# The last experts' rows transposed by DMA from SyncE instead of by TensorE and VectorE

## The reference

```python
x = x + _L0_xattn_ref(_layernorm(x), ctx_1024, ...)
x = x + _L0_ffn_ref(_layernorm(x), ...)
x = x + _L1_xattn_ref(_layernorm(x), ctx_1024, ...)
x = x + _L1_ffn_ref(_layernorm(x), ...)

def _L1_ffn_ref(x, router_w, router_b, w1, b1, w2, b2):
    x_flat = x.reshape(-1, Dx)
    probs = jax.nn.softmax(x_flat @ router_w.T + router_b, axis=-1)
    topk_prob, topk_idx = jax.lax.top_k(probs, K)          # K = 2
    y = jnp.zeros_like(x_flat)
    for e in range(E):                                      # E = 8
        gate = jnp.sum(jnp.where(topk_idx == e, topk_prob, 0.0), axis=-1)
        h = jax.nn.gelu(x_flat @ w1[e].T + b1[e])
        out = h @ w2[e].T + b2[e]
        y = y + gate[:, None] * out
```

## Time and profile before

| | |
|---|---|
| median of 3 runs | 703.61 us (700.66 to 711.06) |
| the profiled execution | 701.29 us, of which the span is 699.6 us |
| busy in the span | PE 550.0 us (79%), DVE 540.8 (77%), POOL 378.3 (54%), ACT 375.6 (54%) |
| the last mixture's slots | first turn at 462.5 us, last scatter issued at 688.7 us |

### The profile page before, as it was taken

How to read it: one execution, slowest core, us unless ns; L and a number is a source line. 1 busy time by engine, 2 the same in 40 slices (tenths; PEclk the granted TensorE clock), 3 DMA queues, 4 the chain that set the end, 5 groups by cost and what they waited for, 6 DMA issues and landing times.

```text
span 699.6 us, 17811 instructions
## 1 busy us (share of the span) xinstructions
PE 550.0 (79%) x6572; PEld 499.8 (71%) x6572; DVE 540.8 (77%) x1063; ACT 375.6 (54%) x556; POOL 378.3 (54%) x324
## 2 busy tenths in 40 slices
PE   6799999999997614897770655159999999999990
PEld 5798989898995503776550444159999999999990
DVE  3678999999997773887655898768888888888860
ACT  1665577777765513997642677305444444444440
POOL 8057698889887306654307883043444554444331
PEclk9899999999998955999995799559999999999996
DMA  8300111212121235897745342421333233333221
GB/s 295 123 2 23 40 56 60 63 54 75 40 77 51 76 122 158 254 315 232 200 145 176 106 111 71 137 61 22 54 51 48 47 48 53 55 48 49 32 27 21
DMA packets 38756, 64.35 MB, mean 92 GB/s; under 512 B 7665, under 2 KB 28786, under 8 KB 38418
## 3 DMA queue, kind: packets, MB, share of 16 engines
q1 hardware_dynamic: 27442, 42.71, 19.2%
q0 software_dynamic: 11232, 20.50, 15.4%
HBM read 45.74 MB, written 17.45 MB: 90 GB/s over the span
## 4 chain that ended last, share of the span: by engine, by line
PE 49%; DVE 22%; issue 7%; DMA 7%; ACT 7%; POOL 5%; DVEq 1%; SPq 0%; ACTq 0%; POOLq 0%
PE banks L1334 46%; DMA sorted_y<-slot_region 3%; POOL rv L526 2%; PE banks L1543 2%; DVE w_region L972 1%; DVE heads L964 1%; DVE slot_region L1212 1%; DMA staging<-w_t 1%; ACT w_region L639 1%; DVE heads L947 1%; DVE w_region L954 1%; DVE w_region L977 1%; DVE w_region L926 1%; POOL wb_region L601 1%; DVE x_res L1279 1%
## 5 line engine op out<-in xcount | busy, mean ns | idle before, releaser
L1334 PE MATMUL banks<-w_region 128*128 128x128 f16 (+6 forms) x1964 | 163.9, 242 | 21.2 <-DVE w_region L1142 9.1
L1334 PEld LDWEIGHTS banks<-w_region 128*128 128x128 f16 (+3 forms) x1964 | 150.0, 118 | 30.4 <-issue 10.2
L614 POOL DMA_INDIRECT out<-slot_region,lg x39 | 65.0, 1667 | 114.4 <-ACT slot_region L823 111.4
L1334 PE MATMUL banks<-w_region,wb_region 128*128 (+1 forms) x1000 | 119.8, 277 | 6.8 <-DMA wb_region<-wk 6.7
L1334 PEld LDWEIGHTS banks<-w_region,wb_region 128*128 128x128 f16 (+1 forms) x1000 | 100.7, 107 | 17.4 <-issue 7.5
L1334 PE MATMUL banks<-slot_region,staging 128*128 128x128 f16 x1872 | 113.1, 221 | 0.1
L785 ACT ACTIVATE wb_region<-wb_region 128x1024 f32<-128x1024 f32 x39 | 41.3, 1058 | 133.0 <-DVE wb_region L1194 133.0
L1334 PEld LDWEIGHTS banks<-slot_region,staging 128*128 128x128 f16 x1872 | 108.5, 99 | 0.2 <-issue 0.2
L1185 DVE COPY staging<-w_region 128x2048 f16 x78 | 60.1, 773 | 35.8 <-PE banks L1334 34.3
L570 POOL DMA_INDIRECT slot_region<-normed_rows,index x46 | 48.1, 1045 | 48.9 <-DVE index L1157 20.5
L1334 PE MATMUL banks<-wb_region,w_region 128*128 (+1 forms) x344 | 50.4, 296 | 13.6 <-DVE slot_region L1212 13.4
(11 more groups left out here) (244 smaller groups left out, 1052.8 us busy)
## 6 DMA issues: line engine op xcount, KB each, us to landing
staging<-w_t SPq DMA_DIRECT2D x24, 512.0 KB, 4.7
sorted_y<-slot_region SPq DMA_DIRECT2D x23, 256.0 KB, 5.6
w_region<-w_t SPq DMA_DIRECT2D x8, 512.0 KB, 5.5
x_res<-x SPq DMA_DIRECT2D x4, 512.0 KB, 9.9
staging<-w_in SPq DMA_DIRECT2D x4, 512.0 KB, 3.7
normed_rows<-w_region SPq DMA_DIRECT2D x16, 128.0 KB, 1.7
staging<-w_out SPq DMA_DIRECT2D x4, 512.0 KB, 3.7
gated_rows<-wb_region SPq DMA_DIRECT2D x16, 128.0 KB, 2.3
```

The source lines that it names most:

```text
L614: g.indirect_dma_start(out=out, out_offset=bass.IndirectOffsetOnAxis(ap=back[:, j:j + 1], axis=0), in_=m.y[:, j % m.YB, 0, :], in_offset=N ...
L1334: return t.matmul(o, a, b, start=start, stop=stop)
```

## The change

The transpose of step 2 is taken from TensorE and VectorE. SyncE issues four DMA transposes for each slot instead, each of one 128 x 128 piece of f16 (32 KB), from the gathered home straight into `m.xT`, which now has three homes (`XB`) in place of two; the gathered rows have seven homes in place of eight and lie behind `m.xT` in the region. SyncE waits for the slot's gather, and from slot 3 on for the end of up of three slots before, whose home it writes. TensorE's up waits for a new semaphore per home (`slot_turned`), VectorE computes the gates as soon as the gather has landed (`slot_gate`), and POOL reuses a home of gathered rows when its gates are computed and its transposes have landed. The first mixture keeps its transposes on TensorE.

```diff
-            m.RING, m.AHEAD, m.YB = ((3, 2, 3), (8, 4, 4))[layer]
-            m.rows, at = carve(SLR, 0, [m.RING, m.A, (2 * D, ROW1)[layer]], F16)
-            m.xT, at = carve(SLR, at, [2, 2 * DC, m.SW], F16)
+            m.RING, m.AHEAD, m.YB = ((3, 2, 3), (7, 4, 4))[layer]
+            m.XB = (2, 3)[layer]
+            m.xT, at = carve(SLR, 0, [m.XB, 2 * DC, m.SW], F16)
+            m.rows, at = carve(SLR, at, [m.RING, m.A, (2 * D, ROW1)[layer]], F16)
...
+        def turned(j):
+
+            n = moes[1].XB
+            return sem(f"slot_turned{j % n}"), 16 * 2 * DC * (j // n + 1)
...
             sp.dma_start(rows_v[1][:, :, D:D + 2].bitcast(F32).rearrange("t p k -> p t k"), token_gates).then_inc(sem("gates_kept"), 16)
+            sp.wait_ge(sem("gates_kept"), 16)
+            m = moes[1]
+            for j in range(m.NSLOT):
+                sp.wait_ge(*gathered(1, j))
+                if j >= m.XB:
+                    sp.wait_ge(*up_done(1, j - m.XB + 1))
+                for c in range(2 * DC):
+                    sp.dma_start(m.xT[:, j % m.XB, c, :], m.rows[:, j % m.RING, 0, c * P:(c + 1) * P],
+                                 transpose=True).then_inc(turned(j)[0], 16)
+            sp.wait_ge(sem("y_scattered"), 16 * NSLOTS[1])
...
-                        pool.wait_ge(sem("slot_cols" if layer else "slot_tr"), made(layer, j - m.RING + 1))
+                    if j >= m.RING and layer == 0:
+                        pool.wait_ge(sem("slot_tr"), j - m.RING + 1)
+                    elif j >= m.RING:
+                        pool.wait_ge(sem("slot_gated"), j - m.RING + 1)
+                        pool.wait_ge(*turned(j - m.RING))
...
-            def slot_cols(j):
+            def slot_gate(j):
                 m = moes[1]
-                dve.wait_ge(sem("slot_tr"), made(1, j + 1))
-                if j >= 2:
-                    dve.wait_ge(*up_done(1, j - 1))
+                dve.wait_ge(*gathered(1, j))
...
-                       in1=pair[:, 0:1], op0=ALU.mult, op1=ALU.add)
-                v.tensor_copy(m.xT[:, j % 2], slot_columns(m, j)).then_inc(sem("slot_cols"), 1)
+                       in1=pair[:, 0:1], op0=ALU.mult, op1=ALU.add).then_inc(sem("slot_gated"), 1)
...
-                pe.wait_ge(sem("slot_cols"), made(1, j + 1))
+                pe.wait_ge(*turned(j))
...
-                xT, ps = m.xT[:, j % 2], hidden(m, j)
+                xT, ps = m.xT[:, j % m.XB], hidden(m, j)
...
-                        slot_tr(layer, s)
+                        if layer == 0:
+                            slot_tr(layer, s)
```

More of the change, by code:

```diff
@@ L566, in gather_rows @@
                 for a in range(m.A):
-                    if j >= m.RING:
-                        pool.wait_ge(sem("slot_cols" if layer else "slot_tr"), made(layer, j - m.RING + 1))
+                    if j >= m.RING and layer == 0:
[3 more added lines that the diff above has]
+                        pool.wait_ge(*turned(j - m.RING))
                     q = m.A * j + a
@@ L1245, in slots_of_last @@
                             slot_weights(0, a)
-                        slot_cols(0)
+                        slot_gate(0)
                     elif s + 1 < n:
-                        slot_cols(s + 1)
+                        slot_gate(s + 1)
                         expert_at(s + 1)
```

## The result

The changed kernel takes **714.7 us** (median of 4 runs, 713.84 to 718.91) against 704.08 of the kernel before in the same comparison: a ratio of 1.0137, 95% interval 1.0093 to 1.0180. It was forecast at 695 and is slower. The profiled execution has a span of 713.2 us, 13.6 more than before.

A forecast was written before the change was run, and what follows sets the result against it. TensorE was taken to be full and to bound the last mixture's slots. The sum was 701.29 - 8.1 (transposes off TensorE) + 1.5 (start) = 694.7 us, predicted as 695, with a range of 692 to 712.

The forecast's parts named there:

- the price of a transpose: SyncE in the last mixture's slots: about 0.45 us per DMA transpose, so a slot's four occupy 1.8 of 5.30 us.
- t: Time of one DMA transpose on SyncE, taken as about 0.45 us; four must fit in 5.30 us, 1.33 each.
- the transposes set the pace: Rival: over 1.33 us per transpose, slots go at SyncE's pace; beyond 1.34 slower than before; 788 us at 1.9. Chance 0.17.
- The 696.5: Estimated total in place of 694.7 if a DMA transpose takes the skill's 1309 ns, four taking 5.24 us.
- Transposes off TensorE: Last mixture's slots: 0.22 us of turns leaves the path 37 times, 8.1 us gained, a slot taking 5.30 for 5.52.
- nothing is gained: Rival: the 0.22 us return as a wait between down and up, leaving only the start's loss, 703 us. Chance 0.05.
- The copy off VectorE: 39 copies of 0.41 us leave VectorE, which has slack in each slot: worth nothing on the path.
- The start: First up of the last mixture waits for four transposes: 1.5 us later, bounds 0.8 to 5.5.
- Latency covered by three homes: Transposes have 13.2 us between issue and use, transfers land after 1.9 to 5.0: covered after the first slots.
- The scatters as a rival: Transposes on the shared DMA engines delay POOL's chained scatters, which then set the slots' pace: 709 or 731 us. Chance 0.12.
- x: Time the transposes add to each scatter's landing; slots then go at 4.5 + x, over 5.52 us beyond x = 1.0.

The follow-up runs named there:

- e1: Changed kernel with a slot's four transposes issued as one instruction of 128 x 512: 696.28 us, ratio 0.9915 to the kernel before.
- e2: Changed kernel with six homes for turned rows in place of three, and eight for gathered rows: 716.34 us, ratio 1.016 to the kernel before.
- e4: Kernel before, with its TensorE turns kept, plus the 156 DMA transposes into homes that no engine reads: 707.02 us, ratio 1.0057 to the kernel before.

## Why the prediction was wrong

**The step that failed** is the price of a transpose. The prediction took "about 0.45 us, the row of the same size on the same queue", for t. Measured is 1.24 us at the median and 1.42 from one to the next. The row it was taken from the earlier trace rows shows plain copies, and a transpose on the same queue holds SyncE almost three times as long. The bounds held it (0.32 to 1.9), and so did the rival *the transposes set the pace*, which put the turning point at t = 1.34 and had a chance of 0.17. By its formula the last slot is turned at 462.5 + 156 x 1.42 = 684.0, and the last up did begin at 685.26. That the two lie so close is in part chance, since the last four ups wait for no transpose.

The margin was thin, and by this working two parts of t were needed to cross it. At 1.234 + 0.04 us, four transposes are 5.10 us, still under 5.30. The 25 longer ones add 21.4 / 39 = 0.55 us to a slot, which makes 5.65 (measured 5.67). That TensorE waits before 17 ups only fits this; no run has four transposes per slot without any fetch. The prediction did not have the program's fetches at all.

The Trainium skill, VectorE: DVE Perf Modes, section "The three transpose paths", has 1309 ns for a 128 x 128 transpose of bf16 by DMA. The trace agrees in size: 1234 ns of issue at the median, for f16. By that figure alone, as an estimate, four take 5.24 us, under the 5.30 of the matmuls, and the kernel would have gained; the longer transposes, of which the section says nothing, turned that. The 696.5 that the prediction gives for this figure does not follow its own terms: with 462.5 + 3 x 1.309 + 2.3 = 468.7 the start is 4.1 us later, and the sum 697.3. And it is no price by area, since 128 x 512 took 1190 ns.

*Transposes off TensorE: 8.1 us.* Right. In e1 up of slot 3 begins at 480.25 and up of slot 38 at 665.75, 5.30 us a slot; in the kernel before it was 5.52. The step of 5.31 us in the earlier trace rows was the right one to read, and the rival that nothing is gained falls with e1.

*The copy off VectorE: nothing.* Not tested by itself. In e1 the chain in the steady slots does not touch VectorE.

*The start: 1.5 us.* Too small, for the same reason. The first four transposes go out from 462.31 to 466.07, 1.25 us apart instead of 0.44, and up begins 2.98 us after the last, at 469.05, **4.4 us** later than the 464.64 of the earlier trace rows. The landing was also longer than the 2.3 us taken. In e1, with one instruction, the first up begins at 465.20, 0.6 us later. The rows of the changed kernel and of e1:

```profile
469.05 4.20 PE L1350 MATMUL banks<-slot_region,staging 128*128 128x128 f16 x48 [11.08 <-DMA slot_region<-slot_region]
```

```profile
465.20 4.36 PE L1349 MATMUL banks<-slot_region,staging 128*128 128x128 f16 x48 [7.51 <-DMA slot_region<-slot_region]
```

*Latency covered by three homes.* Right, by e1: with three homes no up but the first waits for a transpose, and it is SyncE that waits, up to 4.9 us. In e2 SyncE had no wait for a home, so six homes could not show it.

*The scatters as a rival.* They do not set the pace. By the rule of the Trainium skill, DMA: Bandwidth & Descriptors, section "Issuing engines are not separate DMA queues", x should be above zero. In e4 the median landing rises from 3.9 to 4.0 us and the longest from 4.9 to 6.8, and the slots keep their 5.52, so here it is too small to matter.

With 1.19 us for a whole slot, the prediction's sum comes true: 694.7 forecast for the profiled execution, 695.31 with e1 (median 696.28), which beats both kernels. Its start costs 1.6 us by up of slot 3 (480.25 against 478.64).

## What to carry to other kernels

Work that is moved off a full engine onto a queue has a price in that queue's issue time, and here it was paid by the instruction: count instructions per round and compare with the round of the engine that was relieved. Where the trace has no row for an instruction, a row of another kind on the same queue is no price (here it was a lower bound); if the bounds straddle the turning point, as here 0.32 and 1.9 do around 1.34, the forecast should not rest on one end. And before the work is split into pieces that fit a tile, see whether one instruction takes them all.

## What the runs showed of the hardware

- SyncE is held by a DMA transpose between two places of SBUF for 1.19 to 1.25 us at the median, for 128 x 128, 128 x 256 and 128 x 512 f16 alike. The plain transfers of the earlier trace rows hold it for 0.32 and 0.44 us.
- A transpose that is issued while 16 KB of program are fetched often takes longer: 25 long ones in the changed kernel are 0.85 us longer on average, the longest 3.14 us in all. With one transpose per slot, 4 of 39 were over 1.4 us, each beside a fetch. Why a fetch of about 1.1 us holds the issue stays open. Plain transfers may be held too: of the 23 stores at L435 in the kernel before, with a median of 0.43 us, the longest takes 2.08 and stands beside a fetch, but one of 0.33 us at L423 beside another fetch is not longer.
- 39 slots' transposes raise the share of the DMA engines from 0.32 to 0.45 (0.46 in e4, where the scatters' median landing is 4.0 us for 3.9).
